# Rows of x scattered into a table of slots, and fixed first blocks with plain loads, in a two-layer decoder on one Trainium2 core

## The chip, the cores and the metric

One Trainium2 chip, of which the kernel uses one core. The core has five engines that run side by side, each in the order of its own program: PE (TensorE) does matrix products and transposes, DVE (VectorE) and ACT (ScalarE) elementwise work, POOL (GpSimd) elementwise work and the issue of indirect DMAs (gathers and scatters by a table of indices), SP (SyncE) issues plain DMAs. Engines wait for each other by semaphores. The metric is the time of one execution on the device in microseconds (us), the median of several runs.

## The reference

Six sublayers, each `x = layernorm(x + f(x))`, on x of 8 batches x 256 rows x 256 columns in float32: causal attention, a cosine cross-attention, a ternary feed-forward net, linear attention, cross-attention, and at the end a mixture of experts. The last is the one that the change touches:

```
gate_scores = softmax(xf @ gate_w)                    # 2048 rows, 8 experts
topk_scores, topk_idx = top_k(gate_scores, 2)
topk_scores = topk_scores / sum(topk_scores)
h = gelu(einsum('td,edf->etf', xf, w1) + b1)          # 256 -> 1024
y = einsum('etf,efd->etd', h, w2) + b2                # 1024 -> 256
out = einsum('kt,ktd->td', topk_scores.T, y[topk_idx.T, tok])
```

## The kernel before

The stages run in order A, B, C (the first layer), D and E interleaved by batch (linear attention, and cross-attention with the routing that follows it: "the gated stage" of the change's name), F (the experts) and G (the weighted sum of each row's two results, layernorm, output). By the trace D and E run from about 640 us to 1152 us, F from 1178 us to 1457 us, G to the end.

**Order of the work in D and E.** `de_steps` (lines 104 to 120) gives each item a first round and the rounds of its steps. Every engine goes through the same list `DE`, sorted by round, and does what is its own. The items of E: `EPRE` (projections), `PAIR` (scores of two heads: PE makes them, DVE takes the row maxima, `topE`, and subtracts them, `shiftE`, PE turns the result over, ACT takes the exponential into the buffer `staging`, POOL clamps it at line 634, PE multiplies by v at L1132), `EDR` (collects heads: DVE `ctxtok_E`, PE turns it over, ACT and DVE split it) and `EFIN`, the end of a batch: 0 and 1 output projection, sum, layernorm (DVE mean and variance, POOL the power -1/2 at L420 into `lnE_rstd`, DVE L425, ACT L434 writes `x_tok`), 4 the store of the batch's rows to `x_rows` by SP, 5 the router product, 6 softmax and top 2 of 8, 7 the slot of every (row, choice): expert x 2048 + rank of the row within the expert (DVE L1782). Then, still step 7, POOL issues 4 indirect DMAs (L649), each of which scatters 128 codes of 4 bytes (row number, plus 2048 for the second choice) into the table `slot_codes` in DRAM at these slots. POOL handles the two of these jobs in one queue, so that what stands behind the scatters, clamps and L420 of the next batch, waits until they are issued.

**Between E and F** ("the junction"). F works in 23 blocks of 256 rows that each belong to one expert. DVE counts from the totals per expert (lines 1787 to 1819) how many blocks each has, and makes `row_i` (which stretches of `slot_codes` make up the blocks) and `wrow_i` (which expert's weights each block needs). POOL waits for the codes of all batches to be written, gathers `block_codes` (23 x 256, L654), then the weights `w1raw` and `w2raw` of block 0 (128 rows of 2056 and 2304 floats). DVE casts the codes to float (L1821), PE turns them over (L394), DVE makes row numbers `token_i` and output slots `slot_i` of them (L1824 to L1831), POOL gathers the rows of block 0 from `x_rows` into `xg` (two gathers of 128 rows), PE turns them over, ACT and DVE split them into a high and a low part (L1454, L1844), and the first product of F runs at L386. Blocks 1 and 2 are gathered in the same way behind block 0.

**F.** Block j has 4 quarters q; n = 4j + q counts them. For a quarter PE does the first product (`h`, 12 matmuls at L386 to L388), ACT the gelu (L1471), DVE the split of the result (`gh`, L1858 and L1860), and PE, three quarters behind, the second product (`y`, L1214). ACT, DVE and POOL split the weights of quarter n + 3 into high and low parts (ACT L1443 and L1446, DVE L1836 and L1838, POOL L679). `gather_weights` and `gather_x` fetch block j + 3 at q = 2 of block j. At the end of a block POOL scatters the results to `y_rows` (L706). **G** loads `y_rows` by SP as `yc` when all scatters are done.

## Time and profile before

| | us |
|---|---|
| median of 3 runs (lowest, highest) | 1501.17 (1498.74, 1502.59) |
| the profiled execution, its own time | 1496.94 |
| its span, first to last instruction | 1495.1 |
| PE busy | 1315.9 (88%) |
| DVE busy | 917.5 (61%) |
| POOL busy | 794.2 (53%) |
| ACT busy | 572.6 (38%) |
| mean granted clock of PE | 0.937 of full speed |

All times inside the program are from the start of the span of the one profiled execution; 1.84 us of its time lie outside the span. In a row of a timeline stand the start, the length, the engine, the line, the operation with what it writes and reads, and in brackets how long the engine stood idle before it and what ended that. A `bank` is a piece of the accumulation memory that PE writes. The chain of waits is followed back from the last instruction: at each step to what released it, or to the instruction before it on the same engine. Durations of POOL are rough.

### The profile page before, as it was taken

The page shows a single profiled execution, that of the slowest core. Times are in us where ns is not written, and L with a number is a line of the kernel's source. Part 1 is how long each engine was busy: PE and PEld are TensorE (multiplying, and loading weights), DVE is VectorE, ACT ScalarE, POOL GpSimd, SP SyncE. Part 2 cuts the span into 40 slices and gives each one's busy share as a digit, 9 for nine tenths or more (in the row PEclk, how much of TensorE's full clock was granted, in tenths as well). Part 3 has the DMA queues.
Part 4 walks back from the last instruction along what each step waited for, and adds up shares of the span by engine and source line. Part 5 has one row for each costly group of instructions (what it writes and reads, how often), then busy time and mean ns, then how long its engine had stood idle before and what let it go on. Part 6 is the DMA issues. An engine that isn't in the chain of part 4 may idle for free.

```text
span 1495.1 us, 23092 instructions
## 1 busy us (share of the span) xinstructions
PE 1315.9 (88%) x9071; PEld 1117.8 (75%) x9071; DVE 917.5 (61%) x1729; ACT 572.6 (38%) x1171; POOL 794.2 (53%) x762
## 2 busy tenths in 40 slices
PE   6996999999999999968798998898784599999990
PEld 6995788888888888846566666666653499999990
DVE  4665522632442362234577777777794499999986
ACT  3666211211121121123344444444341467676652
POOL 4443666666566576423223335345543678888742
PEclk9997999999999999999899999999795699999995
DMA  5100333333233233111233124134400765666515
GB/s 174 39 17 6 103 99 120 87 99 97 84 114 96 74 113 99 50 41 52 91 119 113 42 98 113 38 102 104 130 14 14 268 219 219 231 225 248 199 49 169
DMA packets 58044, 163.23 MB, mean 109 GB/s; under 512 B 10598, under 2 KB 26185, under 8 KB 50000
## 3 DMA queue, kind: packets, MB, share of 16 engines
q1 hardware_dynamic: 45760, 100.13, 22.8%
q0 software_dynamic: 12176, 61.63, 11.6%
q8 instruction: 72, 1.18, 0.4%
q14 instruction: 36, 0.29, 0.1%
HBM read 136.47 MB, written 27.08 MB: 109 GB/s over the span
## 4 chain that ended last, share of the span: by engine, by line
PE 69%; DVE 17%; ACT 5%; issue 3%; DMA 2%; POOL 2%; SPq 1%; another core or an unknown queue 1%; ACTq 0%; POOLq 0%; DVEq 0%
PE bank L386 15%; PE bank L388 15%; PE bank L387 15%; PE bank L1214 8%; PE bank L394 4%; PE bank L975 3%; DVE topE L1717 3%; DVE shiftE L1726 3%; PE bank L1056 2%; PE bank L1132 2%; PE bank L1043 1%; ACT x_tok L434 1%; DVE topE L1720 1%; SPq L715 1%; DVE x_tok L1881 1%
## 5 line engine op out<-in xcount | busy, mean ns | idle before, releaser
L1590 DVE CAST hid_hi<-bank 128x512 fp32r<-128x512 f32 x96 | 66.4, 691 | 251.9 <-ACT bank L1329 250.8
L518 POOL TENSOR_TENSOR wpiece_lo<-wraw,wpiece_hi 128x1024 fp32r<-128x1024 f32 x88 | 211.0, 2397 | 7.4
L386 PE MATMUL bank<-hid_hi,wpiece_lo 128*128 128x512 f32 x512 | 199.2, 389 | 0.0
L387 PE MATMUL bank<-hid_lo,wpiece_hi 128*128 128x512 f32 x512 | 199.2, 389 | 0.0
L388 PE MATMUL bank<-hid_hi,wpiece_hi 128*128 128x512 f32 x512 | 199.2, 389 | 0.0
L516 POOL TENSOR_SCALAR wpiece_hi<-wraw 128x1024 fp32r<-128x1024 f32 x88 | 94.0, 1068 | 156.7 <-PE bank L388 128.8
L1329 ACT ACTIVATE bank<-bank,ffn_scales 128x512 f32<-128x512 f32 x64 | 42.4, 662 | 301.4 <-PE bank L388 301.4
L634 POOL TENSOR_SCALAR staging<-staging 128x1024 f32<-128x1024 f32 x64 | 66.6, 1042 | 117.1 <-ACT staging L1414 114.9
L386 PEld LDWEIGHTS bank<-hid_hi,wpiece_lo 128*128 128x128 f32 x512 | 96.1, 188 | 20.2
L387 PEld LDWEIGHTS bank<-hid_lo,wpiece_hi 128*128 128x128 f32 x512 | 96.1, 188 | 19.9
L388 PEld LDWEIGHTS bank<-hid_hi,wpiece_hi 128*128 128x128 f32 x512 | 96.1, 188 | 19.9
L386 PE MATMUL bank<-xgT_hi,w_lo 128*128 128x256 f32 x368 | 107.3, 291 | 2.7 <-DVE xgT_lo L1844 2.7
L1414 ACT ACTIVATE staging<-bank 128x512 f32<-128x512 f32 x128 | 69.7, 595 | 103.9 <-PE bank L1132 72.1
L387 PE MATMUL bank<-xgT_lo,w_hi 128*128 128x256 f32 x368 | 105.1, 286 | 0.0
L388 PE MATMUL bank<-xgT_hi,w_hi 128*128 128x256 f32 x368 | 105.1, 285 | 0.0
L1214 PE MATMUL bank<-w_hi,gh_lo 128*128 128x256 f32 x368 | 104.1, 283 | 0.0
L1214 PE MATMUL bank<-w_lo,gh_hi 128*128 128x256 f32 x368 | 104.1, 283 | 0.0
L1214 PE MATMUL bank<-w_hi,gh_hi 128*128 128x256 f32 x368 | 104.1, 283 | 0.0
L1471 ACT ACTIVATE bank<-bank,w1raw 128x256 f32<-128x256 f32 x184 | 74.8, 444 | 76.4 <-PE bank L388 75.0
L1056 PE MATMUL bank<-feat 64*128 64x256 f32 (+1 forms) x512 | 61.6, 362 | 33.1 <-DVE shiftE L1726 25.7
L1699 DVE TENSOR_TENSOR aw<-bank,mask_d 128x768 f32<-128x768 f32 x64 | 60.9, 953 | 47.4 <-PE bank L1056 44.1
L1717 DVE TENSOR_REDUCE topE<-bank 128x4 f32<-128x1024 f32 x64 | 77.8, 1215 | 16.5 <-PE bank L1111 16.3
(337 smaller groups left out, 3727.5 us busy)
## 6 DMA issues: line engine op xcount, KB each, us to landing
wraw<-in_C_w SPq DMA_DIRECT2D x88, 512.0 KB, 3.6
split_qk<-qk_hi SPq DMA_DIRECT2D x64, 128.0 KB, 2.4
split_qk<-qk_lo SPq DMA_DIRECT2D x64, 128.0 KB, 2.4
xt_lo<-split_qk SPq DMA_DIRECT2D x8, 1024.0 KB
xt_hi<-split_qk SPq DMA_DIRECT2D x8, 1024.0 KB
yc<-y_rows SPq DMA_DIRECT2D x16, 256.0 KB, 5.9
ctx_raw<-in_ctxT SPq DMA_DIRECT2D x16, 192.0 KB, 3.4
xraw<-in_xT SPq DMA_DIRECT2D x8, 256.0 KB, 3.4
```

Source lines behind the costliest of these rows:

```text
L386: pe.e.matmul(o, sl, mh, start=start and i == 0, stop=False)
L387: pe.e.matmul(o, sh, ml, start=False, stop=False)
L388: made = pe.e.matmul(o, sh, mh, start=False, stop=stop and i == n - 1)
L516: pool.mark(pool.e.tensor_scalar(pair[0], raw, 1.0, 0.0, ALU.mult, ALU.add))
L518: pool.e.tensor_tensor(pair[1], raw, f(pair[0]), ALU.subtract).then_inc(done, 1)
L634: pool.e.tensor_scalar(pr, pr, 1.0, 0.0, ALU.min, ALU.max).then_inc(s_prob, 1)
L1056: made = pe.e.matmul(o, ft[rows, k, 1, t * P:(t + 1) * P], ft[rows, k, 0, t * P:S], start=True, stop=True)
L1214: made = pe.e.matmul(u.ap[:, t * D:(t + 1) * D], hh[:, i, st], ww[:, i, :], start=fc == 0 and k == 0 and t == 0, stop=fc == FC - 1 and k == 2,
L1414: act.e.activation(prob_e[n % 3][:, i, :, :], u.ap[:, :].rearrange("p (k s) -> p k s", k=TT), ACT.Exp, scale=scale_e).then_inc(u.drained, 1)
L1471: made = act.e.activation(u.ap[:, cols], u.ap[:, cols], ACT.Gelu, bias=w1raw[j % 4][:, c:c + 1])
L1590: dve.mark(dve.e.tensor_copy(hi[:, o, :], u.ap[:, :]))
L1717: dve.mark(dve.e.tensor_reduce(top[:, :], scores, AX.X, ALU.max))
```

## The change

A second table in DRAM, `x_slots` (8 experts x 2048 slots x 256 floats), holds rows of x themselves, at the same slots as the codes.

- While C runs, SP fills the first 256 slots of each expert from the input x, 8 DRAM-to-DRAM transfers of 256 KB, so that slots which no row takes hold finite numbers.
- `EFIN` gets a ninth step. In step 7 POOL now issues 4 indirect DMAs that scatter 128 rows of x, 1 KB each, into `x_slots`; the 4 scatters of codes move to step 8, one round later.
- Blocks 0 to 7 of F are now the first 256 slots of expert 0 to 7, whatever the counts. Their weights are loaded by SP with plain DMAs (`first_weights`), those of blocks 0 and 1 during E, once D's buffers are free; their rows are loaded by SP from `x_slots` (`first_x`). The other 15 blocks (`NMORE`) hold what experts have beyond 256 rows and are gathered by POOL as before. 23 blocks remain 23.
- The codes are loaded in two pieces, `first_codes` (8 x 256, by SP) and `more_codes` (15 x 256, by POOL's gather), and PE, DVE turn them into `slot_i` and `token_i` in `row_codes`, at block 1, quarter 0 (`CODES_AT`) and no longer ahead of F. 
- DVE splits the weights of n = 0 and 1 ahead of its counts; ACT runs one small gelu after the last router exponential. Tiles in on-chip memory are laid out in another order, `l_yc` reuses semaphores.

On POOL, in the last two batches of E and at the start of F, before (`seen` is the running count per expert, `route` and `shares` belong to the routing, `staging` rows are the clamps):

```order
404 L649 DMA slot_codes<-codes,slot 16640x1 x4
405 L634 TENSOR_SCALAR staging<-staging 128x1024 x5
406 L420 TENSOR_TENSOR lnE_rstd<-lnE_rstd,minus_half 128x2
407 L634 TENSOR_SCALAR staging<-staging 128x1024 x3
...
413 L649 DMA slot_codes<-codes,slot 16640x1 x4
414 L420 TENSOR_TENSOR lnE_rstd<-lnE_rstd,minus_half 128x2
415 L649 DMA slot_codes<-codes,slot 16640x1 x4
416 L654 DMA block_codes<-slot_codes,row_i 23x256
```

and the same place now:

```order
409 L674 DMA x_slots<-x_tok,slot 16384x256 x4
410 L658 TENSOR_SCALAR staging<-staging 128x1024
411 L680 DMA slot_codes<-codes,slot 16640x1 x4
412 L658 TENSOR_SCALAR staging<-staging 128x1024 x4
413 L433 TENSOR_TENSOR lnE_rstd<-lnE_rstd,minus_half 128x2
...
420 L674 DMA x_slots<-x_tok,slot 16384x256 x4
421 L680 DMA slot_codes<-codes,slot 16640x1 x4
422 L433 TENSOR_TENSOR lnE_rstd<-lnE_rstd,minus_half 128x2
423 L674 DMA x_slots<-x_tok,slot 16384x256 x4
424 L680 DMA slot_codes<-codes,slot 16640x1 x4
```

There are eight scatters instead of four ahead of the next batch's power (L420, now L433), with one clamp between the two groups of four where clamps are due.

On DVE, around the fourth and fifth quarter of F (n = 3, the last of block 0, and n = 4), now; the seven rows 1033 to 1039 are `row_codes`, which stood ahead of all splits before:

```order
1029 L1933 CAST gh_hi<-bank 128x512
1030 L1935 TENSOR_TENSOR gh_lo<-bank,gh_hi 128x512
1031 L1858 TENSOR_TENSOR w_lo<-w1raw,w_hi 128x512
1032 L1860 TENSOR_TENSOR w_lo<-w2raw,w_hi 128x256
1033 L1873 CAST first_codes_f<-first_codes 8x256
1034 L1873 CAST more_codes_f<-more_codes 15x256
1035 L1876 COPY code_f<-bank 128x46
```

They now stand behind `gh` of n = 3 and the split of n = 6. On PE the transposes of the two code tables stand ahead of the first product of n = 4 and so behind the second product of n = 1:

```order
4160 L1277 MATMUL bank<-w_hi,gh_hi 128x256
4161 L407 MATMUL bank<-ident,first_codes_f 128x8
4162 L407 MATMUL bank<-ident,more_codes_f 128x15
4163 L407 MATMUL bank<-ident,first_codes_f 128x8
4164 L407 MATMUL bank<-ident,more_codes_f 128x15
4165 L399 MATMUL bank<-xgT_hi,w_lo 128x256
```

PE can go on with n = 4 only when DVE has come to its rows 1033 and 1034. SP's queue at the junction holds, in this order, the rows and weights of the first blocks and then the codes:

```order
135 L739 DMA xg<-x_slots 128x2x256 x2
136 L739 DMA w1raw<-in_F_w 128x2056
137 L739 DMA w2raw<-in_F_w 128x2304
138 L739 DMA xg<-x_slots 128x2x256
139 L739 DMA w1raw<-in_F_w 128x2056
140 L739 DMA w2raw<-in_F_w 128x2304
141 L739 DMA xg<-x_slots 128x2x256
142 L739 DMA first_codes<-slot_codes 8x256
```

Six transfers of weights and rows stand between the first two `xg` and the codes. The diff, cut to its core:

```diff
+CODES_AT = (1, 0)
-        items.append((e + 13, 5, "EFIN", (b,), (0, 1, 2, 4, 4, 5, 7, 8)))
+        items.append((e + 13, 5, "EFIN", (b,), (0, 1, 2, 4, 4, 5, 7, 8, 9)))
...
                     elif step == 7:
                         if b < B - 1:
                             add_seen(pool, b)
-                        pool.wait_ge(w_empty, 16)
+                        pool.wait_ge(w_empty, 16 * (1 + NE))
                         pool.wait_ge(s_slot, b + 1)
+                        pool.wait_ge(s_x["E"], b + 1)
+                        for t in range(TT):
+                            for j in range(TOPK):
+                                pool.e.indirect_dma_start(
+                                    x_slots, bass.IndirectOffsetOnAxis(ap=slot[b % 2][:, t, j:j + 1], axis=0),
+                                    x_tok[:, b * TT + t, :], None).then_inc(w_slots, 16)
+                    elif step == 8:
                         for t in range(TT):
                             for j in range(TOPK):
...
-            pool.wait_ge(s_frow, 1)
-            for i in range(2):
-                pool.wait_ge(w_codes[i], 16 * 4 * (B // 2))
-            gather(block_codes[:, :], slot_codes.rearrange("(r s) one -> r (s one)", s=BT), row_i[0:NBK, 0:1], l_bc)
-            gather_weights(0)
-            gather_x(0)
-            for j in (1, 2):
-                gather_weights(j)
-                gather_x(j)
             for n in range(AHEAD):
                 split_w(n)
             for name, step, (j, q) in FS:
                 n = j * NQ + q
                 if step == 0:
-                    if q == 2 and j + 3 < NBK:
+                    if (j, q) == (0, 1):
+                        pool.wait_ge(s_frow, 1)
+                        for i in range(2):
+                            pool.wait_ge(w_codes[i], 16 * 4 * (B // 2))
+                        gather(block_codes[1][:, :], slot_codes.rearrange("(r s) one -> r (s one)", s=BT), row_i[0:NMORE, 0:1], l_bc)
+                    if q == 2 and NE <= j + 3 < NBK:
                         gather_weights(j + 3)
                         gather_x(j + 3)
...
                 piece(m)
+                if 2 * NPIECE <= m < 2 * NPIECE + NE:
+                    load(first_rows(m - 2 * NPIECE), a["x"][:, 0:BR, :], w_empty)
...
+                    if (b, step) == (B - 1, 2):
+                        last = use["D", "o", b]
+                        sp.wait_ge(last.drained, last.done)
+                        for j in range(2):
+                            first_weights(j)
...
+            sp.wait_ge(s_slot, B)
+            sp.wait_ge(w_slots, 16 * 4 * B)
+            first_x(0)
+            first_x(1)
+            for j in range(2, NE):
+                if j == 4:
+                    for i in range(2):
+                        sp.wait_ge(w_codes[i], 16 * 4 * (B // 2))
+                    load(block_codes[0][:, :], slot_codes[0:NE * B * S].rearrange("(e s) one -> e (s one)", e=NE)[:, 0:BT], l_codes)
+                first_weights(j)
+                first_x(j)
...
+                    if (j, q) == CODES_AT:
+                        u = use["F", "i"]
+                        pe.wait_ge(s_codes, 2)
...
+                        if b == B - 1:
+                            act.e.activation(top_e[0][:, :], minus_half[:, :], ACT.Gelu)
...
+                            dve.wait_ge(w_slots, 16 * 4 * b)
...
+            for n in range(AHEAD - 1):
+                split_w(n)
             u = use["F", "n"]
...
                 if step == 0:
+                    if (j, q) == CODES_AT:
+                        row_codes()
```

## Rows read from the trace of the kernel before

**Rows 1.** Chain of waits from E's end into F: start, length, what.
```profile
1140.23 0.73 POOL lnE_rstd L420
...
1155.98 6.50 DMA slot_codes<-codes,slot
...
1163.44 3.79 DMA block_codes<-slot_codes,row_i
```
**Rows 2.** Timeline of PE at the junction and at n = 4.
```profile
1175.99 1.12 PE L394 MATMUL bank<-ident,xg 128*128 128x128 f32 x4 [8.00 <-DMA xg<-x_rows,token_i]
1178.52 0.58 PE L386 MATMUL bank<-xgT_hi,w_lo 128*128 128x256 f32 x1 [1.41 <-DVE xgT_lo L1844]
...
1190.31 0.28 PE L386 MATMUL bank<-xgT_hi,w_lo 128*128 128x256 f32 x1
```
**Rows 3.** Windows: from:to, length, busy of PE, PEld, DVE, ACT, POOL, clock, DMA share, GB/s.
```profile
1077.00:1082.00 5.00, 4.63 (x33) 3.07 (x34) 4.86 (x8) 2.52 (x5) 1.04 (x1) 0.66 0.31 34
...
1152.00:1178.00 26.00, 1.52 (x6) 1.00 (x6) 9.02 (x41) 3.15 (x6) 13.91 (x14) 0.50 0.42 149
...
1174.00:1176.00 2.00, 0.01 (x1) 0.01 (x1) 0.05 (x1) 0.71 (x2) 1.41 (x2) 0.50 0.94 357
...
1230.00:1300.00 70.00, 70.00 (x588) 70.00 (x587) 67.63 (x106) 48.48 (x99) 58.53 (x60) 1.00 0.62 228
```
**Rows 4.** Timeline of POOL, scatters and L420 behind batches 2 and 3.
```profile
990.22 0.73 POOL L420 TENSOR_TENSOR lnE_rstd<-lnE_rstd,minus_half 128x2 f32<-128x2 f32 x1 [3.37 <-DVE lnE_rstd L414]
...
1035.62 0.96 POOL L649 DMA_INDIRECT slot_codes<-codes,slot  x1 [0.30 <-issue]
1036.88 0.95 POOL L649 DMA_INDIRECT slot_codes<-codes,slot  x1 [0.30 <-issue]
...
1039.04 0.72 POOL L420 TENSOR_TENSOR lnE_rstd<-lnE_rstd,minus_half 128x2 f32<-128x2 f32 x1
```
**Rows 5.** Timeline of POOL behind batches 4, 5, 6 and at the junction.
```profile
1074.29 0.72 POOL L420 TENSOR_TENSOR lnE_rstd<-lnE_rstd,minus_half 128x2 f32<-128x2 f32 x1
...
1103.60 3.06 POOL L634 TENSOR_SCALAR staging<-staging 128x1024 f32<-128x1024 f32 x3
...
1140.23 0.72 POOL L420 TENSOR_TENSOR lnE_rstd<-lnE_rstd,minus_half 128x2 f32<-128x2 f32 x1 [1.51 <-DVE lnE_rstd L414]
...
1155.98 0.95 POOL L649 DMA_INDIRECT slot_codes<-codes,slot  x1 [0.30 <-issue]
```
**Rows 6.** Timeline of DVE, where it takes L420's result.
```profile
992.64 0.25 DVE L425 SCALAR_TENSOR_TENSOR lnE_mv<-lnE_mv,lnE_rstd 128x2 f32<-128x2 f32 x1
...
1041.45 0.15 DVE L425 SCALAR_TENSOR_TENSOR lnE_mv<-lnE_mv,lnE_rstd 128x2 f32<-128x2 f32 x1
...
1077.24 0.15 DVE L425 SCALAR_TENSOR_TENSOR lnE_mv<-lnE_mv,lnE_rstd 128x2 f32<-128x2 f32 x1
```
**Rows 7.** Timeline of PE behind batches 3 and 5.
```profile
1042.48 0.66 PE L394 MATMUL bank<-ident,ctxtok_D 128*128 128x128 f32 x4 [1.28 <-DVE ctxtok_D L1657]
...
1077.37 0.54 PE L1111 MATMUL bank<-xt_lo,xt_hi 64*128 64x256 f32 x4 [3.17 <-DVE shiftE L1726]
...
1106.38 1.07 PE L1132 MATMUL bank<-staging,v_e 128*32 128x256 f32 x16
```
**Rows 8.** DMA issues of the page: KB each, median us to landing.
```profile
yc<-y_rows SPq DMA_DIRECT2D x16, 256.0 KB, 5.9
...
xraw<-in_xT SPq DMA_DIRECT2D x8, 256.0 KB, 3.4
```
**Rows 9.** Chain of waits at the end of F: a scatter of rows of 1 KB.
```profile
1460.24 2.10 DMA y_rows<-yblock,slot_i
```
**Rows 10.** Timeline of DVE: last row of the counts, code cast, split of n = 6.
```profile
1158.20 0.24 DVE L1819 TENSOR_SCALAR wrow_i<-expert_of,row_no 128x23 uint32<-128x23 f32 x1
1167.25 0.28 DVE L1821 CAST block_codes_f<-block_codes 23x256 f32<-23x256 uint32 x1 [8.81 <-DMA block_codes<-slot_codes,row_i]
...
1192.92 0.95 DVE L1838 TENSOR_TENSOR w_lo<-w2raw,w_hi 128x256 fp32r<-128x256 f32 x1
```

183 lines of the change are left out of this document (109 added, 74 removed).

## The prediction

> **What bounds the kernel now.** I read the windows first, to see where PE has no slack. In F it has none: over 1230 to 1300 us PE is busy for all 70 us and DVE for 67.6 of them [rows 3]. The change takes no product away (23 blocks before, 23 after), so F keeps its length. At the junction PE is busy for 1.5 us of 26 [rows 3]. That is the stretch in which time can be had, and the chain of waits says what fills it. The last scatter of codes is issued at 1155.98 and lands 6.50 us later; the gather of the block codes takes 3.79 us [rows 1]; DVE casts them at 1167.25 [rows 10]; two gathers of x follow, PE turns the rows over at 1175.99, and F's first product starts at 1178.52 [rows 2]. Then I read POOL's timeline in E, since the change puts 28 scatters more there ahead of other work (the 4 of batch 7 are dealt with below). The rows to look at are those of L420, the power in the layernorm of the next batch: what POOL had in front of it, and when DVE (L425) wanted its result.
>
> **The junction, gain.** In the new kernel the last 4 scatters on the path carry rows of x, at the same place and with the same issue cost: a scatter of 4-byte codes occupies POOL for 0.96 us and the next begins 1.26 us later [rows 5, 4], and a scatter of rows into y_rows is of the same kind. So the last is again issued at 1155.98, on the old clock. How long it takes to land no row of E shows. From below, the last scatter of 1 KB rows in F took 2.10 us [rows 9], perhaps with part of its rows dropped; from above, the codes took 6.50 [rows 1]. The thing scattered is like the first, the crowd of transfers like the second; I take 3.5, nearer to the first, so 1159.5. SP then loads block 0's rows, 256 KB. Plain loads of that size took 3.4 us in the median (xraw), 5.9 (yc, in a crowd) [rows 8]. I take 3.4: 1162.9. From PE's transposes of the gathered rows to the first product 1178.52 - 1175.99 = 2.53 us passed [rows 2]: 1165.4. The gain is 1178.5 - 1165.4 = 13.1 us. Its ends: 2.1 and an estimated 2.7 give 15.2; 6.5 and 5.9 give 7.6.
> By the Trainium skill (DMA: Bandwidth & Descriptors, Specifications) a transfer under 512 B makes the engine read, modify and write, which would explain 6.50 us for codes and speak for the short landing of 1 KB rows; by its formula of 2.0 us plus bytes over 436 GB/s (Anatomy of one DMA) 128 KB would land in 2.3 us, an estimate, and the sum would be 1.2 us better. Against the change the same page says (Issuing engines are not separate DMA queues) that SP's loads run on the same 16 engines as POOL's gathers; the gain above is not from quicker transfers but from the two that fell out of the chain.
>
> **What must be ready by 1165.4.** The weights of blocks 0 and 1 are loaded during E, behind D's last product. DVE splits n = 0 and 1 (2 x (0.69 + 0.42), an estimated 2.2 to 4.4 us) and then runs the counts, which ended at 1158.44 before [rows 10]: 1160.6 to 1162.9, so 1.5 us of cover in the worse case, and a cost of what exceeds it. ACT's table load moves ahead of the junction. POOL's 4 scatters of codes for batch 7 end 5.1 us later, at 1162.0, in front of splits of w2 that PE's second product wants 7.5 us after the first. All hidden.
>
> **E, cost.** Four more scatters per batch hold POOL for 4 x 1.26 = 5.1 us [rows 4], in front of clamps and of L420. I go batch by batch.
> - Behind batches 0, 1, 2 POOL waited for DVE ahead of L420, 3.37 us at 990.22, and DVE took the result at 992.64 [rows 4, 6]; 990.95 + 5.1 - 3.37 = 992.7. Cost about 0.
> - Behind batch 3 POOL had no wait: L420 ran from 1039.04 to 1039.76 [rows 4]; now to 1044.86. DVE wanted it at 1041.45 [rows 6] and all that DVE does later stands behind it, ctxtok_D at once, for which PE was already waiting at 1042.48 [rows 7]. Cost 3.4.
> - Behind batch 4: L420 ends at 1075.01 [rows 5], now 1080.1; DVE wanted it at 1077.24 [rows 6]. Cost 2.9.
> - Behind batch 5 clamps stand there, three from 1103.60 on [rows 5]; the second ended near 1105.6, now 1110.8 (one clamp fits between the groups). PE's L1132 at 1106.38 needs it [rows 7]: up to 4.4 for PE, but DVE had work on its queue that doesn't depend on it. I take 1.5, between 0 and 4.4.
> - Behind batch 6 L420 at 1140.23 is itself in the chain of waits [rows 1], with 1.51 us of idle time ahead of it [rows 5]. 5.1 - 1.5 = 3.6, in full, since PE, DVE and ACT all have nothing but this batch left.
> Sum 3.4 + 2.9 + 1.5 + 3.6 = 11.4 us; the bounds are 3.6 (only batch 6) and 14.3, with 1 for the early batches 15.3. Batch 7's scatters of x take the place of its codes and cost nothing; the new wait of DVE for w_slots ahead of the top 2 asks for scatters issued over 20 us earlier.
>
> **F's fifth quarter, cost.** PE now waits there for DVE's two casts. PE came to n = 4 at 1190.31, 11.8 us after its first product [rows 2]. DVE ended the split of n = 6 at 1192.92 + 0.95 = 1193.87 [rows 10], 15.35 after it. DVE running late there cost nothing before, because PE wants those parts two quarters later. Now PE stands until 15.35 + 2 x 0.28 [rows 10] = 15.9, so 4.1 us; if that last split takes the usual 0.42 and its partner 0.68 and not 0.95 and 1.26, 3.0. I take 3.6. It is only this if the codes are there by then: they stand in SP's queue behind x0, x1 and the weights and rows of blocks 2 and 3, 4 x 0.26 + 2 x 2.23 = 5.5 MB, at the 357 GB/s of 1174 to 1176 [rows 3] 15.4 us, plus a landing of 3.4, from 1159.5 on: 1178.3, against DVE's arrival at 1165.4 + 14.2 to 15.4 = 1179.6 to 1180.8. Cover 1.3 us. Bounds of this term: 0 (DVE catches up, since its first splits are done early) and 6.5 (codes 2 to 3 us late).
>
> **Free.** The 8 fills and early weights lie under C's and D's products; 4.2 MB of scattered rows (32 x 128 KB) are spread over all of E; DVE's seven small rows (under 2 us in all) fall into F, where DVE has 2.4 of 70 us free, and G isn't touched.
>
> **Sum.** On the profiled execution 1496.94 + 11.4 - 13.1 + 3.6 = 1498.8 us, plus 1.9. That execution is 4.2 us under the median of the runs shown, which themselves lie 3.9 apart; the difference goes on the median: 1501.17 + 1.9 = 1503.1.
>
> **The rivals.**
> (A) The stages absorb POOL's delay everywhere but behind batch 6, because the engines in E wait for each other in turns and a late DVE row meets a PE that had other work. For it: POOL is only 53% busy, and the waits there are mostly its own. Against: PE waited directly on DVE at 1042.48 and 1077.37 [rows 7]. 3.6 + 3.6 - 13.1 = -5.9: 1495.3, with the shortest landings 1493.
> (B) The other side: PE's clock. At 1077.37 PE had stood 3.17 us [rows 7] and the granted clock over 1077 to 1082 was 0.66, so part of it at the lower level of 1.2 GHz [rows 3]; the gap of 1.28 at 1042.48 is the one the change makes 4.6. If the gaps behind batches 3 and 5 and the one at n = 4 each bring 5 us at half clock, each costs 2.5 more: 1.9 + 7.5 = +9.4: 1510.6. It decides once gaps reach about 3 us, if PE then has dense work and the chain runs through it.
> (C) The scattered rows land as slowly as the codes and the load is crowded: the gain is 7.6 and not 13.1, so +7.4: 1508.6.
> (D) The change does not do what it says for the codes: taken off the path ahead of F, they return as a wait inside it. If SP's queue is served at F's mean 228 GB/s [rows 3], 5.5 MB take 24 us, the codes land at 1187, PE stands some 7 us longer: +8.9: 1510.1. It decides from a rate under some 320 GB/s.
> By the Trainium skill (DMA: Bandwidth & Descriptors, Queues, rings and completion order) each DMA engine takes descriptors in the order of its ring, which is why the small load would wait for all weights ahead of it; no row of the kernel before shows a small load behind large ones.
>
> **How the numbers follow.** A measurement here tells about 0.3% (4.5 us) from no change. The forecast has a chance of 0.34, A 0.34, B 0.14, C 0.10, D 0.08. Faster by over 0.3% (under 1496.7): 0.25 of A and 0.04 of the forecast, 0.29. Slower (over 1505.7): 0.09 of the forecast and 0.25 of B, C, D, 0.34. Same 0.37. The bounds of the terms, 3.6 to 15.3, 7.6 to 15.2 and 0 to 6.5, give 1489.6 to 1515.4 when all are at their ends; the ends don't come together, and 1491 to 1511 leaves out about 2 in 10. For the forecast alone 1499 to 1507.
>
> **What would show it.** Junction: the first product of F 13 us nearer to the issue of batch 7's last first-group scatter (22.5 us before, 9.4 expected), x_slots landing in 2 to 6.5 us in the chain. E: L433 behind batches 3, 4 and 6 each with eight scatters in front of it and DVE's L438 waiting for POOL about 3.4, 2.9 and 4.4 us, and batch 7's last scatter of x issued at about 1167.4 (its counterpart stood at 1155.98). F: a wait of PE of 3 to 4 us ahead of first_codes_f, released by DVE and not by a DMA. I would be wrong if that scatter comes at 1160 or earlier (A), if PE's clock in E falls under what it was (B), or if the DVE cast waits for the load of first_codes (D).

## The result, and the profile after

The changed kernel takes 1520.91 us (median of 6 runs, 1517.45 to 1522.55), the kernel before beside it 1501.88 (6 runs, 1498.74 to 1509.05). The ratio is 1.0119 with a 95% interval of 1.0095 to 1.0143: **slower by 1.2%**, 18 us. All ratios in this document are of executions in the chip's fast state alone, and they are not the quotients of the medians printed beside them. The forecast was 1503.1 and its range ended at 1511, so it was wrong.

The profiled execution has a span of 1519.1 us, before 1495.1, so 24.0 us are to be accounted for. The medians are 19.0 apart: the profiled execution of the kernel before was 4.9 us under its median, so about a fifth of the 24 lies in which execution was profiled. From the page of the kernel after (section 1, then section 2's clock, then the chain by engine), and last the chain by engine of the kernel before:

```profile
PE 1319.8 (87%) x9073; PEld 1121.7 (74%) x9073; DVE 911.3 (60%) x1729; ACT 574.5 (38%) x1172; POOL 795.2 (52%) x762
...
PEclk9997999999999999988999999998787699999995
...
PE 67%; DVE 13%; POOL 7%; issue 5%; ACT 4%; DMA 3%; SPq 2%; ACTq 0%; POOLq 0%; DVEq 0%
```
```profile
PE 69%; DVE 17%; ACT 5%; issue 3%; DMA 2%; POOL 2%; SPq 1%; another core or an unknown queue 1%; ACTq 0%; POOLq 0%; DVEq 0%
```

POOL is as little busy as before, yet its share of the chain of waits went from 2% to 7%. A share of busy time would have shown nothing; the chain does.

To see where the 24 us came in, I took the same instruction in both timelines and subtracted the starts:

| instruction | before | after | lag |
|---|---|---|---|
| DVE, first row of the layernorm of D's first batch | 695.99 | 701.62 | +5.6 |
| the same, E's first batch | 823.80 | 828.57 | +4.8 |
| E, batch 4 | 1041.45 | 1054.79 | +13.3 |
| E, batch 5 | 1077.24 | 1097.01 | +19.8 |
| E, batch 6 | 1119.41 | 1143.41 | +24.0 |
| first scatter of batch 7 | 1152.11 | 1178.43 | +26.3 |
| F's first product | 1178.52 | 1194.36 | +15.8 |
| PE, transposes of x for block 3 | 1208.03 | 1231.84 | +23.8 |
| last scatter into `y_rows` | 1460.24 | 1479.10 | +18.9 |
| last DVE row of G | 1490.92 | 1509.74 | +18.8 |
| end of the span | 1495.1 | 1519.1 | +24.0 |

The lag is how much later the row starts than in the kernel before. So the terms are: +4.8 ahead of E's batches (e_part, e_part_late and before_pad, below, in which nothing is changed ahead of E, show 7.4, 1.6 and 2.2 at this row, so a lag of this size comes without the change), **E +21.5, junction -10.5, the fifth quarter +8.0, the rest of F -4.9, the end of the program +5.2**.

**E.** Timeline of POOL behind batch 3 (L674 scatters rows, L680 codes, L433 is the power), kernel after:

```profile
1043.03 1.11 POOL L674 DMA_INDIRECT x_slots<-x_tok,slot  x1 [0.50 <-issue]
...
1046.98 0.96 POOL L674 DMA_INDIRECT x_slots<-x_tok,slot  x1 [0.30 <-issue]
1047.98 1.05 POOL L658 TENSOR_SCALAR staging<-staging 128x1024 f32<-128x1024 f32 x1
1049.21 0.99 POOL L680 DMA_INDIRECT slot_codes<-codes,slot  x1 [0.18 <-issue]
...
1053.03 0.96 POOL L680 DMA_INDIRECT slot_codes<-codes,slot  x1 [0.30 <-issue]
1054.01 0.74 POOL L433 TENSOR_TENSOR lnE_rstd<-lnE_rstd,minus_half 128x2 f32<-128x2 f32 x1
```

Eight scatters and a clamp stand in one piece of 11 us ahead of the power. DVE and PE, kernel after, where they want what POOL makes; the brackets are the idle time ahead of the row and what ended it:

```profile
1054.79 1.01 DVE L438 SCALAR_TENSOR_TENSOR lnE_mv<-lnE_mv,lnE_rstd 128x2 f32<-128x2 f32 x1 [4.47 <-POOL lnE_rstd L433]
...
1097.01 1.01 DVE L438 SCALAR_TENSOR_TENSOR lnE_mv<-lnE_mv,lnE_rstd 128x2 f32<-128x2 f32 x1 [4.48 <-POOL lnE_rstd L433]
...
1167.29 0.16 DVE L438 SCALAR_TENSOR_TENSOR lnE_mv<-lnE_mv,lnE_rstd 128x2 f32<-128x2 f32 x1 [4.49 <-POOL lnE_rstd L433]
```
```profile
1056.68 1.11 PE L407 MATMUL bank<-ident,ctxtok_D 128*128 128x128 f32 x4 [6.89 <-DVE ctxtok_D L1726]
...
1131.76 1.94 PE L1193 MATMUL bank<-staging,v_e 128*32 128x256 f32 x16 [5.61 <-POOL staging L658]
```

DVE waits for the power behind batches 3, 4 and 6 and PE for a clamp behind batch 5. The first two of these rows also last 1.01 us, where the same row took 0.15 before [rows 6]; a clamp of POOL (1054.73 to 1055.77) runs beside the first of them. Before, the first two rows of DVE had no wait in front at all [rows 6], and PE's 6.89 was 1.28 [rows 7]. Behind two of these stands PE's clock is low, where it wasn't before. Windows behind batches 3 and 5, columns as in [rows 3], kernel after and then kernel before:

```profile
1056.60:1062.00 5.40, 5.32 (x31) 3.60 (x32) 1.31 (x4) 2.40 (x6) 1.04 (x1) 0.50 0.41 82
...
1131.70:1137.00 5.30, 5.24 (x32) 3.42 (x33) 1.35 (x2) 2.30 (x5) 2.05 (x3) 0.50 0.00 0
```
```profile
1041.00:1045.00 4.00, 2.51 (x26) 1.68 (x28) 2.64 (x8) 2.54 (x5) 1.22 (x2) 1.00 0.60 55
...
1106.00:1112.00 6.00, 3.77 (x38) 2.41 (x36) 5.86 (x9) 3.05 (x6) 2.21 (x3) 1.00 0.00 0
```

0.50 is the lower level, 1.2 GHz, after PE had stood 6.9 and 5.6 us.

**The junction.** SP and POOL, kernel after: the last scatter of rows, and SP's load of them, issued as soon as they have landed. Then PE:

```profile
1182.49 0.96 POOL L674 DMA_INDIRECT x_slots<-x_tok,slot  x1 [0.30 <-issue]
```
```profile
1184.97 0.87 SPq L739 DMA_DIRECT2D xg<-x_slots  x2
```
```profile
1191.84 1.11 PE L407 MATMUL bank<-ident,xg 128*128 128x128 f32 x4 [13.84 <-DMA xg<-x_slots]
1194.36 0.58 PE L399 MATMUL bank<-xgT_hi,w_lo 128*128 128x256 f32 x1 [1.41 <-DVE xgT_lo L1866]
...
1212.22 0.27 PE L407 MATMUL bank<-ident,first_codes_f 8*128 8x8 f32 x1 [6.58 <-DVE more_codes_f L1873]
```

The rows land in 2.48 us (1182.49 to 1184.97), their load takes 6.87 (to 1191.84), and 2.52 pass to the first product: 11.87 us from the last scatter on, where 22.54 stood before (1178.52 - 1155.98) [rows 1, 2].

**The fifth quarter.** The last row above is the new wait inside F: PE stands for 6.58 us. Behind it the chain of waits, kernel after, and DVE's row:

```profile
1187.54 12.62 DMA slot_codes<-codes,slot
1200.22 11.44 DMA first_codes<-slot_codes
```
```profile
1211.68 0.28 DVE L1873 CAST first_codes_f<-first_codes 8x256 f32<-8x256 uint32 x1 [1.43 <-DMA first_codes<-slot_codes]
```

DVE came to the cast at 1210.25 and still waited 1.43 for the codes. Their last scatter took 12.62 us to land and the load of 8 KB another 11.44. It landed at 1211.66, 0.2 us behind the rows of block 3, which SP had issued ahead of it at 1190.95 and which took 20.5 us. And PE's clock, in the windows around it (columns as in [rows 3]):

```profile
1205.00:1212.00 7.00, 0.64 (x6) 0.43 (x4) 5.50 (x11) 1.25 (x3) 0.72 (x1) 0.80 0.83 311
1212.00:1216.00 4.00, 3.78 (x19) 3.74 (x20) 1.05 (x6) 0.28 (x1) 0.00 (x0) 0.50 0.36 150
```

After the stand of 6.6 us PE works at 0.50, the level of 1.2 GHz, for the 4 us looked at. The stand makes the first product of n = 4 come 6.7 us later after F's first than before (18.5 against 11.8); the other 1.3 of the 8.0 come behind it.

**The end.** SP's waits at the last line, kernel after and then kernel before:

```profile
SPq L190 <- PEq L190: 5.6, 1, 5.6
```
```profile
SPq L186 <- PEq L186: 0.5, 1, 0.5
```

SP waits 5.6 us for PE's queue, once, at the program's last line; before it was 0.5.

**The rest of F.** Timeline of PE, before and then after, at the transposes that open each block:

```profile
1315.61 0.60 PE L394 MATMUL bank<-ident,xg 128*128 128x128 f32 x4
...
1327.56 0.60 PE L394 MATMUL bank<-ident,xg 128*128 128x128 f32 x4
```
```profile
1314.39 0.60 PE L407 MATMUL bank<-ident,xg 128*128 128x128 f32 x4
...
1326.15 0.60 PE L407 MATMUL bank<-ident,xg 128*128 128x128 f32 x4
```

PE is busy without a gap at clock 1.00 in both. Over 15 blocks a block takes 11.95 us before (1219.98 to 1399.28) and 11.79 after (1231.84 to 1408.62). The 19 blocks behind block 3 make 3.2 us of that 0.17. The next block took 13.5 us before, since PE waited in it, timeline of PE before:

```profile
1406.94 0.39 PE L386 MATMUL bank<-xgT_hi,w_lo 128*128 128x256 f32 x1 [1.31 <-DVE xgT_lo L1844]
```

The kernel after has no such wait there. 3.2 and 1.6 make 4.8 of the 4.9.

### The profile page after: what moved, and what is told of

Same layout as the page of the kernel before. It is cut to its first block, busy times and chain, and to the rows that moved or that the text cites. A ratio compares the mean times of both kernels' runs of the same rounds, so it can differ in the third digit from the quotient of the medians.

```text
span 1519.1 us, 23135 instructions
## 1 busy us (share of the span) xinstructions
PE 1319.8 (87%) x9073; PEld 1121.7 (74%) x9073; DVE 911.3 (60%) x1729; ACT 574.5 (38%) x1172; POOL 795.2 (52%) x762
## 4 chain that ended last, share of the span: by engine, by line
PE 67%; DVE 13%; POOL 7%; issue 5%; ACT 4%; DMA 3%; SPq 2%; ACTq 0%; POOLq 0%; DVEq 0%
PE bank L399 15%; PE bank L400 15%; PE bank L401 14%; PE bank L1277 8%; PE bank L407 4%; PE bank L1036 3%; POOL x_slots L674 2%; DVE topE L1786 2%; DVE shiftE L1795 2%; PE bank L1117 2%; POOL slot_codes L680 2%; SPq L739 2%; PE bank L1193 1%; PE bank L1104 1%; ACT x_tok L447 1%
## 5 line engine op out<-in xcount | busy, mean ns | idle before, releaser
L707 POOL TENSOR_TENSOR w_lo<-w2raw,w_hi 128x256 fp32r<-128x256 f32 x92 | 78.0, 865 | 37.9 <-ACT w_hi L1515 37.3
```

Of the source, the lines that this page charges most:

```text
L707: pool.e.tensor_tensor(w2[n % 6][1][:, 1, :], w2_cols(*divmod(n, NQ))[:, 1, :], f(w2[n % 6][0][:, 1, :]), ALU.subtract).then_inc(s_w2lp, 1)
```

## The experiments

Medians come from runs beside the kernel before on one chip; chips and hours differ, so only ratios are compared, and differences within one set. The diffs are cut ("..."), and the comments in them are mine.

| kernel | median, us (runs) | before beside it | ratio, 95% |
|---|---|---|---|
| after2, the change again | 1531.21 (4) | 1513.54 | 1.0114 (1.0063 to 1.0165) |
| e_part, E's part alone | 1534.1 (4) | 1513.54 | 1.0131 (1.0083 to 1.0179) |
| late, scatters behind the power | 1504.78 (4) | 1513.54 | 0.9943 (0.9894 to 0.9992) |
| cast, codes half a block later | 1524.58 (4) | 1513.54 | 1.0059 (1.0003 to 1.0115) |
| codes_first, groups exchanged | 1523.18 (4) | 1512.66 | 1.0123 (1.0055 to 1.0191) |
| both, late and cast | 1502.96 (10) | 1512.66 | 0.9945 (0.9915 to 0.9975) |
| both_xfirst | 1505.78 (10) | 1512.66 | 0.9971 (0.9933 to 1.0009) |
| both_one | 1501.8 (10) | 1512.66 | 0.9946 (0.9911 to 0.9981) |
| e_part_late | 1512.2 (10) | 1506.73 | 1.0016 (0.9973 to 1.0058) |
| groups | 1499.79 (10) | 1506.73 | 0.9946 (0.9915 to 0.9977) |
| rows_first | 1504.09 (10) | 1506.73 | 0.997 (0.9937 to 1.0003) |

Two kernels, after_pad and before_pad, ran once each. The theories were: that E costs by the **place** of the scatters, ahead of the power that DVE waits for (called P in the expectations), against their number or the bytes they move; that the junction's load is slow because of what is on the DMA engines beside it; that the stall in the fifth quarter is DVE's and the codes' lateness; and, for the end, guesses that each had one kernel.

### after2: the change once more

> The changed kernel once more, beside the others on one chip. 1518 to 1523. Its trace tells which of the lags come back: the 3.5 us that D's start lost to a lower clock (650 to 690 us), PE's gap of 2.6 us with nothing to wait for at 1008.8, and the 5.6 us at the very end in which the program waits for PE's sequencer. What is bound to the program comes back; what is chance does not.

1.0114 against 1.0119. The loss is the kernel's and not that of one set of runs (the absolute times are those of another chip, so 1518 to 1523 was missed). Of the three things that its trace was to tell, the 5.6 us at the end and the gap near 1010 us are there again; the late start of D is not (the row that lagged 5.6 us at D's first batch lags 1.1).

### e_part: E's part alone

```diff
-        items.append((e + 13, 5, "EFIN", (b,), (0, 1, 2, 4, 4, 5, 7, 8)))
+        items.append((e + 13, 5, "EFIN", (b,), (0, 1, 2, 4, 4, 5, 7, 8, 9)))
...
+                        for t in range(TT):
+                            for j in range(TOPK):
+                                pool.e.indirect_dma_start(
+                                    x_slots, ..., x_tok[:, b * TT + t, :], None).then_inc(w_slots, 16)
+                    elif step == 8:
...
+            sp.wait_ge(w_slots, 16 * 4 * B)
...
+                            dve.wait_ge(w_slots, 16 * 4 * b)
```

> The kernel before, with one part of the change alone: in step 7 the 4 scatters of rows of x into x_slots, the scatters of codes in a step 8 one round later. Nobody reads x_slots; the junction and F are those of before. Theory P (POOL's order: eight scatters in front of the next batch's power and clamps): in the changed kernel the lag against before grew by 4.7 and 4.6 us where DVE waits for the power behind batches 3 and 4, 5.4 at the clamps behind batch 5, 3.7 behind batch 6, 18 in all; here the same, and the 4 scatters of batch 7 stand in front of its codes on the path, 5.1 more: plus 20 to 24 us, 1522 to 1525, with D's start (640 to 700 us) as before. Rival Q (the loss in E comes mostly from the fills, the early weights and the new layout of the tiles, or from where PE's clock happens to fall): plus 5 to 12.

The rest of the kernel is that of before, so batch 7's four scatters too are extra here. 20.6 us slower: with nothing else changed, E's part alone costs as much as the whole change. The waits are the same ones, timeline of DVE in e_part:

```profile
1058.62 1.01 DVE L427 SCALAR_TENSOR_TENSOR lnE_mv<-lnE_mv,lnE_rstd 128x2 f32<-128x2 f32 x1 [4.48 <-POOL lnE_rstd L422]
...
1171.30 0.16 DVE L427 SCALAR_TENSOR_TENSOR lnE_mv<-lnE_mv,lnE_rstd 128x2 f32<-128x2 f32 x1 [4.50 <-POOL lnE_rstd L422]
```

SP's wait at the end was 0.5 us here, as before; it comes with the change in F.

### late: all eight scatters behind the next batch's power

```diff
-        items.append((e + 13, 5, "EFIN", (b,), (0, 1, 2, 4, 4, 5, 7, 8, 9)))
+        items.append((e + 13, 5, "EFIN", (b,), (0, 1, 2, 4, 4, 5, 7, 8, 10, 11)))
...
-        w_slots = sem("w_slots")
+        w_slots = ring(2, lambda i: sem(f"w_slots{i}"))
...
+                    elif step == 8:      # rows of x
...
+                    elif step == 9:      # codes
...
-                            dve.wait_ge(w_slots, 16 * 4 * b)
+                            dve.wait_ge(w_slots[b % 2], 16 * 4 * (b // 2))
```

> The changed kernel, with both groups of scatters moved behind the next batch's power: x in round 10 and codes in round 11 of a batch's end (they stood in rounds 8 and 9, the next batch's power stands in round 9), and w_slots kept apart for even and odd batches. Same number of scatters, same bytes. Theory P: DVE's waits of 4.5 us for the power go; POOL has idle time of 2 to 6 us between clamps there, but a group of four is still 5.1 us in front of a clamp: 10 to 16 us come back of the 18: 1505 to 1511. Rival Q: it stays within 4 us of the changed kernel, 1517 to 1523.

26 us faster than after2, beyond the expected gain, and faster than the kernel before. Timeline of POOL in late: the power is first, the scatters behind it, and where the power waits it is POOL that waits, for DVE:

```profile
1151.50 0.72 POOL L433 TENSOR_TENSOR lnE_rstd<-lnE_rstd,minus_half 128x2 f32<-128x2 f32 x1 [6.83 <-DVE lnE_rstd L427]
1152.40 1.09 POOL L675 DMA_INDIRECT x_slots<-x_tok,slot  x1 [0.18 <-issue]
...
1161.40 0.96 POOL L681 DMA_INDIRECT slot_codes<-codes,slot  x1 [0.30 <-issue]
```

The lag against the kernel before, at the first scatter of batch 7, is 11.3 us, 9.4 of which it had at E's first batch: E's own part fell from 21.5 to 1.9, with as many scatters as in the kernel after. That is the best of seven traces of kernels with the rows behind the power, not the typical one (see the part on why the prediction was wrong). The junction got worse: 15.9 us from the last scatter of rows (1167.38) to the first product (1183.29). SP's load, in late, was issued 3.94 us behind the last scatter, and PE had the rows 9.44 later:

```profile
1171.32 0.87 SPq L740 DMA_DIRECT2D xg<-x_slots  x2
```
```profile
1180.76 1.11 PE L407 MATMUL bank<-ident,xg 128*128 128x128 f32 x4 [17.80 <-DMA xg<-x_slots]
...
1199.16 0.27 PE L407 MATMUL bank<-ident,first_codes_f 8*128 8x8 f32 x1 [4.50 <-DVE more_codes_f L1875]
```

### e_part_late: the same on the kernel before

```diff
-        items.append((e + 13, 5, "EFIN", (b,), (0, 1, 2, 4, 4, 5, 7, 8)))
+        items.append((e + 13, 5, "EFIN", (b,), (0, 1, 2, 4, 4, 5, 7, 8, 10)))
...
+                    elif step == 8 and b < B - 1:
+                        # the 4 scatters of rows, for batches 0 to 6 only
```

> The kernel before, with the scatters of rows of x of batches 0 to 6 alone added, and these behind the next batch's power (round 10 of a batch's end); the codes stay where they were, and batch 7 scatters codes alone. In e_part the same 28 scatters (and 4 of batch 7) in front of power and clamps gave plus 20.6 us. Theory P (the place in POOL's queue): plus 0 to 4 us against before, ratio 1.000 to 1.003. Rival T (the transfers themselves, 3.7 MB of rows and their crowding of other loads, cost in E): plus 8 to 14, ratio over 1.005.

1.0016 where e_part had 1.0131. It leaves out batch 7's rows (at 5.1 us, the price of a group of four, they would account for less than half of the difference); the 28 others are all there. So four scatters more per batch cost some 12 to 17 us more ahead of the power than behind it. Behind it their cost isn't told apart from none by the ratio, whose interval ends at 1.0058, 8.7 us, and the medians are 5.5 us apart. The trace isn't free of cost either: batch 7's first scatter of codes lags 9.6 us, 1.6 of them at E's first batch, so E is 8.1 us longer. Part of that is what rival T, the transfers themselves, spoke of: POOL waited 4.5 us for the context (`ctx_raw`, 13.0 us to land) and PE 2.1 for `xt_hi` (12.4), loads that no engine waited for in the kernel before. Timelines of POOL and DVE in e_part_late: power, then rows; DVE's row has no wait:

```profile
1041.75 0.72 POOL L422 TENSOR_TENSOR lnE_rstd<-lnE_rstd,minus_half 128x2 f32<-128x2 f32 x1
...
1043.69 1.06 POOL L657 DMA_INDIRECT x_slots<-x_tok,slot  x1 [0.19 <-issue]
```
```profile
1044.70 0.15 DVE L427 SCALAR_TENSOR_TENSOR lnE_mv<-lnE_mv,lnE_rstd 128x2 f32<-128x2 f32 x1
```

### codes_first: the two groups exchanged

```diff
+                    if (step == 7 and b == B - 1) or (step == 8 and b < B - 1):      # rows of x
...
-                    elif step == 8:
+                    if (step == 8 and b == B - 1) or (step == 7 and b < B - 1):      # codes
```

> The changed kernel with the two groups of scatters exchanged in batches 0 to 6: codes in step 7 (where they stood before the change), rows of x one round later. Same number in front of the same clamps and powers. Theory P (the place in POOL's queue is all): no difference, within 3 us of the changed kernel, ratio to before 1.010 to 1.014. Rival T (part of the loss is in the transfers: the scatters of 4-byte codes now run at the time of the store to x_rows, the load of the context and an instruction load of ACT, where all engines stood for 3 to 5 us near 1010 us): the gap near 1010 goes, minus 4 to 7 us, ratio 1.006 to 1.009.

The ratio, 1.0123, is that of the kernel after, but its interval (1.0055 to 1.0191) also holds the 1.006 to 1.009 of the rival, and the quotient of the medians would be 1.0070. The trace decides for the place: E's own part is 21.1 us (25.0 at batch 7's first scatter, 3.9 at E's first batch), in the kernel after 21.5. It also answers another question: the kernel after has a piece near 1010 us in which ACT waits for something the profile calls remote, which is most of the first stretch's 3.9 us in E (the table in the part on why the prediction was wrong). It is gone there in codes_first, and another has come at 886; the kernel before has one at 880. Timelines of ACT, after, before, codes_first:

```profile
1012.02 1.09 ACT L1477 ACTIVATE staging<-bank 128x512 f32<-128x512 f32 x2 [7.04 <-remote]
```
```profile
880.92 1.09 ACT L1414 ACTIVATE staging<-bank 128x512 f32<-128x512 f32 x2 [9.90 <-remote]
```
```profile
886.82 1.08 ACT L1478 ACTIVATE staging<-bank 128x512 f32<-128x512 f32 x2 [11.99 <-remote]
```

Four more kernels with the E of the kernel after, or nearly so, have it at 1011 to 1017 (cast 8.0 us, after2 8.0, e_part 9.3, after_pad 9.7), and groups too (4.6); in late there is none of over 4 us. So it comes with an order of the work and not by chance, and what it costs is part of E's 21.5; its cause is open.

### cast: the codes wanted half a block later

```diff
-CODES_AT = (1, 0)
+CODES_AT = (2, 0)
+CAST_AT = (1, 2)
...
```

DVE's two casts come at n = 6, PE's transposes and the rest at n = 8.

> The changed kernel, with DVE's two casts of the codes at block 1, quarter 2, and PE's transposes and the rest of the row numbers at block 2, quarter 0, instead of both at block 1, quarter 0. PE then asks for the casts two quarters (5.8 us) after DVE's place for them, more than the 4 us by which DVE runs behind PE, and the codes, which landed 17.3 us after F's first product, are asked for 23.5 us after it. Theory: the stall of 6.6 us and the slow clock behind it (lag 17.3 to 24.1 us from n = 3 to n = 5) go: minus 5 to 7 us against the changed kernel, 1514 to 1516. Rival: the loads of the first blocks hold the codes or the weights back anyway and the wait only moves: minus 0 to 2.

6.6 us faster than after2; the wait ahead of `first_codes_f` is gone. From F's first product to the last scatter into `y_rows` 278.0 us pass, against 284.7 in the kernel after: 6.7, and 8.0 less in the kernel both below (276.8). So moving the casts returns most of the fifth quarter's 8.0 us, wait and slow clock together.

### both: late and cast

The edits of the two.

> The changed kernel with both edits: scatters of a batch behind the next batch's power (as in the run late), and DVE's casts two quarters ahead of PE's transposes of the codes (as in cast). Alone they gave minus 26 and minus 7 us against the changed kernel beside them. Theory: they lie in different stages and add up: minus 30 to 34 against the changed kernel, which is minus 13 to 17 against the kernel before, a ratio of 0.989 to 0.992. Rival: part of the two gains is the same (PE's clock falls less often), and it ends within 3 us of late, ratio 0.993 to 0.995.

The gains don't add: 0.9945, as late alone. In the trace F is shorter by what cast promises (276.8 us against late's 283.6), but the gated stage was longer by nearly as much in that execution: the lag at batch 7's first scatter is 17.4 against late's 11.3, and ACT stood 9.2 us at 912 us for something the profile calls remote, which it didn't in late. With ten runs a ratio is still 0.3%, 4 to 5 us, wide to either side. What became of F's gain in the medians is not settled.

### both_xfirst: weights of blocks 2 and 3 held back until x0 is there

```diff
             first_x(1)
+            sp.wait_ge(l_rows[0], 16)
```

> The kernel both, and SP issues the weights of blocks 2 and 3 only once the rows of block 0 have landed. In the changed kernel those rows (256 KB) took 6.9 us to land, with 4.5 MB of weights issued right behind them, where plain loads of that size had taken 3.4 alone. Theory (the weights crowd the rows out): the rows land in 3.4 to 4.5 us and F's first product comes 2.5 to 3.5 us earlier, minus 2 to 3.5 against both. Rival (what slows the rows is the 4 scatters of codes issued at the same time): they land in 6 to 7 us as before, and the weights 4 us later: 0 to plus 2.

The rows still took 9.3 us. Timeline of SP in both_xfirst, with the next transfer issued when they had landed:

```profile
1171.58 0.87 SPq L741 DMA_DIRECT2D xg<-x_slots  x2
...
1180.84 0.35 SPq L741 DMA_DIRECT2D w1raw<-in_F_w  x1
```

So the weights behind the load were not what slowed it. What was left beside it were batch 7's codes, and ahead of them the eight scatters of batch 6, which end 2 us before those of batch 7 in this kernel as in late and both.

### groups: codes back in step 7, rows behind the power

```diff
+                        (scatter_codes if b < B - 1 else scatter_rows)(b)     # step 7
...
+                        (scatter_rows if b < B - 1 else scatter_codes)(b)     # step 8, round 10
```

with the edit of cast.

> The kernel both, with the codes of batches 0 to 6 back in step 7 (four scatters in front of the next power, as before the change) and only the rows of x behind it; batch 7 as in both. In the trace of both POOL ran 8 scatters of batch 6 right up to those of batch 7, the rows of block 0 landed 9.5 us after their load was issued (6.9 in the changed kernel), and the junction was 3 us longer than in the changed kernel. Theory: the scatters of 4-byte codes are what crowds the junction; with those of batch 6 some 15 us earlier the rows land in 6 to 7 us and F starts 2.5 to 3.5 us earlier than in both: ratio 0.992 to 0.993. Rival: the rows are slow by the scatters of batch 7's codes alone: no change to both, 0.9945.

0.9946 (0.9915 to 0.9977), 7 us faster than the kernel before beside it by the medians; late, both and both_one have 0.9943 to 0.9946 too, so these four aren't told apart, and the ratio is what the rival said. The trace is what the theory said, nearly: the junction takes 12.40 us (landing 2.49, load 7.38), where late took 15.9. E's own part is 4.4 us.

### rows_first: batch 7's codes scattered only after x0 has landed

```diff
-            for n in range(AHEAD):
+            for n in range(AHEAD - 1):
                 split_w(n)
+            pool.wait_ge(l_rows[0], 16)
+            scatter_codes(B - 1)
+            split_w(AHEAD - 1)
```

on groups, with the casts at (2, 0) and the transposes at (2, 2).

> The kernel groups, and POOL issues the 4 scatters of batch 7's codes only when the rows of block 0 have landed; since the codes come later, DVE's casts stand at block 2, quarter 0, and PE's transposes at block 2, quarter 2. Theory: with no scatter of codes beside it the load of block 0's rows takes 3.4 to 5 us and not 7 to 9.5; from the last scatter of rows to F's first product 9 to 10.5 us (14.4 in the changed kernel, 18 in both): minus 4 to 8 us against both, ratio 0.989 to 0.992. Rival (the crowd is the weights, 2.2 MB for block 2 right behind): 0 to minus 1 against groups.

Timelines of POOL, SP and PE in rows_first:

```profile
1178.26 0.96 POOL L629 DMA_INDIRECT x_slots<-x_tok,slot  x1 [0.30 <-issue]
...
1183.68 0.98 POOL L636 DMA_INDIRECT slot_codes<-codes,slot  x1 [3.03 <-DMA xg<-x_slots]
```
```profile
1180.76 0.87 SPq L750 DMA_DIRECT2D xg<-x_slots  x2
```
```profile
1183.46 0.90 PE L408 MATMUL bank<-ident,xg 128*128 128x128 f32 x3 [9.62 <-DMA xg<-x_slots]
1185.99 0.58 PE L400 MATMUL bank<-xgT_hi,w_lo 128*128 128x256 f32 x1 [1.41 <-DVE xgT_lo L1878]
```

The load takes 2.70 us, and the first product comes 7.7 us after the last scatter. That settles the junction. With four scatters of 4-byte elements issued within 4 us of it the load takes 6.9 to 7.5 (after, after2, after_pad, cast, codes_first, groups), 4 to 5 us more, and 9.3 to 9.5 (late, both, both_one, both_xfirst) where batch 6's eight scatters end just ahead too. How they slow it is open: in the 6.9 us of the kernel after the scatters' own packets took 0.4% of the DMA engines' time and the load's queue 74.5%, so it is the load's packets that took longer.

The total didn't follow: 0.997, not told apart from groups. E is written as in groups, but the trace has a lag of 22.2 us at batch 7's first scatter, groups' 11.0, and the profile says where it came from. Timelines of PE and POOL in rows_first:

```profile
892.87 0.80 PE L1184 MATMUL bank<-xt_lo,xt_hi 64*128 64x256 f32 x4 [7.99 <-DMA xt_hi<-split_qk]
```
```profile
1071.32 0.61 POOL L541 TENSOR_SCALAR ctx_hi<-ctx_raw 96x512 fp32r<-96x512 f32 x1 [6.86 <-DMA ctx_raw<-in_ctxT]
```

PE and POOL stand for plain loads, 17.7 us for the 1 MB of `xt_hi` and 15.3 for the context, and over these two places DVE's lag grows by 7.4 and 7.0 us, nearly all of E's 15.1. What happened at the junction seems to happen in E as well, though no kernel isolates it there: where codes are scattered in step 7 beside the load of `xt_hi`, it takes 5.6 to 7.4 us in the median and 12.1 to 17.7 at worst (groups, e_part_late, rows_first); with no scatter beside it 4.8 to 5.0 and at most 6.7 (late, both, both_one, both_xfirst). F is 2.4 us longer than in groups besides (280.5 against 278.1).

### both_one: one tile for all codes

One `block_codes` tile of 23 rows, one cast, two transposes on PE instead of four.

> The kernel both, with the two code tables in one tile of 23 rows, as in the kernel before: one cast and one wait, and PE has two transposes and no longer four, so that its program is as long as that of the kernel before. In four traces of kernels with the whole change the end waited 5.6 us for PE's sequencer, in those of before and e_part 0.5. Theory R (the end waits for a piece of PE's program to be loaded, and it depends on the program's length): the 5.6 fall to 0.5, minus 4 to 5 us against both. Rival (it hangs on something else at the end, such as SP's longer list of last waits): 5.6 again, no difference to both over 1 us.

As both (0.9946), and SP's last wait stayed 5.6 us, so it is not the extra rows and transposes of the codes.

### after_pad and before_pad: 64 products more at the end of PE's program

```diff
+            for i in range(64):
+                pe.e.matmul(last.ap[:, 0:NE], ones_r[:, :], seen[:, :], start=True, stop=True)
```

> The changed kernel with 64 small products added at the very end of PE's program, run while PE is idle in the last stage; nobody reads them. One look. Theory R2 (at the end of the program PE has to load a piece of its instructions, since a border between two pieces happens to lie behind F's last product; the padding makes it cross the border while it is idle): the last wait of 5.6 us for PE's sequencer falls to about 0.5. Rival: it hangs on something else than where PE's program ends: 5.6 again.

> The kernel before with 64 small products added at the very end of PE's program, run while PE is idle in the last stage; nobody reads them. One look. In every kernel with the changed F the end waits 5.6 us for PE's sequencer, in before, e_part and e_part_late 0.4 to 0.5; the padding did not change it in after_pad. If the wait hangs on where PE's program ends at all, it should turn up here: 5.6. If it belongs to something else in the changed F: 0.5.

SP's last wait was 5.6 us in the one and 0.4 in the other, as without the products. It stands in every kernel that has the change in F (eleven of them) and in none that hasn't (before, e_part, e_part_late, before_pad). It is not the length of PE's program. Its cause is open.

## Why the prediction was wrong

The direction of each term was right, and the mechanism of all three in the main; **the sizes were not**. Predicted: +11.4, -13.1, +3.6. Measured in the profiled execution: +21.5, -10.5, +8.0. Then came +5.2 at the end and -4.9 in the rest of F, which it had at nothing, and the 4.8 ahead of E.

**E, 11.4 predicted, 21.5 found.** This term is the largest miss, 10.1 us of the 22.1 between the forecast's +1.9 and the 24.0. By its own steps:

| stretch | predicted | DVE's lag, from and to | net |
|---|---|---|---|
| up to the wait behind batch 3 | 0 | 4.8 to 8.7 | 3.9 |
| behind batch 3 | 3.4 | 8.7, 13.3 behind the wait, 14.2 behind the long row, 16.7 behind the slow clock, 15.2 | 6.5 |
| behind batch 4 | 2.9 | 15.2, 19.8 behind the wait, 20.6 behind the long row, 21.0, 19.2 | 4.0 |
| behind batch 5 | 1.5 | 19.2, 24.6 behind the wait, 22.6 | 3.4 |
| behind batch 6 | 3.6 | 22.6 to 26.3 | 3.7 |

The lags are those of the last row ahead of each wait and of the rows behind it; the nets add up to the 21.5. The four waits come to 18.3 of it, 1.6 times the term. The long row is DVE's first row behind the power, 1.01 us and not 0.15, 0.9 us each time.

The step "up to 4.4 for PE, but DVE had work on its queue that doesn't depend on it. I take 1.5" failed: DVE had none. Timeline of DVE after: it stands itself, for what ACT makes from the late clamp's products.

```profile
1135.64 0.69 DVE L1737 TENSOR_TENSOR ctxT_E_lo<-bank,ctxT_E_hi 128x512 fp32r<-128x512 f32 x1 [5.27 <-ACT ctxT_E_hi L1409]
```

That DVE was busy there before was read as cover. Whether that work stood ahead of the waiting row in DVE's order would have had to be read as well. Behind batches 3 and 4 the price took the old spacing of POOL's rows: but POOL's group began 1.5 us later against DVE than before (its scatters at 1043.03, lag 10.1; DVE's lag 8.7), so the slack was smaller than the rows of the old trace had it. And behind batch 3 the slow clock adds: DVE's next row that hangs on PE (`v_e`, 1047.08 before, 1063.51 after) lags 16.4 us, 2.2 more than the row ahead of it, and later rows 2.5 more, of which 1.5 is caught up. Batch 6, where all had the same one thing left, was right to 0.1. Even the upper bound (15.3) was too low: it had no clock in it, and nothing for the first stretch of the table.

How much of E's loss is the place, thirteen traces tell, one execution each; E's own part is the lag at batch 7's first scatter less that at E's first batch. With eight scatters ahead of the power it is 21.1 to 29.3 us (codes_first 21.1, after 21.5, e_part 22.9, cast 24.6, after2 28.5, after_pad 29.3). With the rows behind the power it is 1.9 to 15.1 (late 1.9, groups 4.4, both_one and both_xfirst 7.4, e_part_late 8.1, both 10.3, rows_first 15.1), and before_pad, which has no such scatters, has 1.4. So the place makes most of the loss and not all of it; what is left behind the power, 7.4 in the middle trace, goes in part to the slow loads and the remote waits named above.

**The junction, -13.1 predicted, -10.5 found.** The landing was 2.5 (predicted 3.5) and the transposes 2.52 (2.53). The step that failed is the load, "I take 3.4": it took 6.87, above even the 5.9 of a crowd [rows 8]. The text had batch 7's four scatters of codes "end 5.1 us later", in front of splits, and counted them on POOL only; they are in flight right beside the load. rows_first shows it at 2.70 without them.
By the Trainium skill (DMA: Bandwidth & Descriptors, Specifications) transfers under 512 B make a DMA engine read, modify and write; 4-byte elements that land in 6.50 us [rows 1], or 12.62 beside F's loads, where 1 KB rows take 2.5 agree with it, but no run here shows what the DMA engines did to them.

**The fifth quarter, +3.6 predicted, +8.0 found.** DVE's arrival was right to half a microsecond: 1210.25 is 15.9 us after the first product, worked out was 15.35. The steps that failed are the cover and the clock: "Cover 1.3 us" for the codes was -1.43, and the clock behind the stand was 0.50, a part of rival B, where the term had no clock. The stand was 6.6 and not 4.1: 1.4 for the codes, 0.5 because DVE came later than worked out, and 0.5 because PE came to it 11.3 us after its first product and not 11.8. The codes were late as rival D had it: the six transfers ahead of them and the two of x0 and x1, 5.5 MB, took from 1184.97 to 1211.45, 26.5 us at about 208 GB/s where the prediction had 15.4 us at 357, and the codes landed 0.2 us behind the last of them. In late, after2 and codes_first too the codes land within 0.2 us of block 3's rows. The prediction also left out that SP waits for `w_codes` and so issues this load only when the last scatter has landed, 12.62 us after its issue; as block 3's rows landed later still, these traces show no cost of it. Moving the casts takes 6.7 to 8.0 of the term back.

**Rivals.** A (the stages absorb it) fell: the lag grows at each of the four places and gives only 1 to 2 us back between them. B was partly right: the clock fell to 0.50 behind batches 3 and 5 and behind the stall at n = 4, the three places it named, once PE had stood 5.6 to 6.9 us; it measured 2.2 to 2.5 us behind batch 3, next to nothing behind batch 5 (the lag grows by 0.1), and 1.3 at n = 4 (8.0 less 6.7), where B had 2.5 each. C (rows land as slowly as codes) fell, 2.5 us, though its second half, the crowded load, was the true one. D had the right place and the right mechanism, and its sign came: DVE's cast waited for the load of `first_codes`. Its size was a fifth of what D had, since DVE arrived 1.43 us before the codes and not some 7.

**Unforeseen.** "F keeps its length" failed: PE's products are the same in number, but each block takes 0.17 us less, 3.2 of the 4.9 us. This goes with the changed F (e_part_late has 11.95 us per block, both 11.8). The change lays the tiles in on-chip memory out in another order; whether that is it was not tried. The 5.2 us at the end go with SP's wait for PE's queue, 5.6 us and not 0.5; why it waits is open.

## What to carry to other kernels

Work that is put on an engine's queue is priced by what waits behind it, not by the engine's busy share: put issues of no hurry behind the next thing another engine waits for, not ahead. When a wait is said to be covered by work of the waiting engine, read in its own order that this work stands ahead of the wait and doesn't depend on it. And count a moved DMA twice, once on the engine that issues it and once against the transfers in flight beside it, above all where its elements are small.
